# Selecting 512 tokens for each of 16 experts: a search and list building written anew, on one Trainium2 core

## The reference

```python
n_tokens = 8192; n_experts = 16; capacity = 512
logits = xn @ router_weight.T + router_bias
probs = softmax(logits, axis=-1)
_, idx = top_k(logits.T, capacity)
...
gates = take_along_axis(probs.T, idx, axis=1)
output = zeros.at[idx].add(y * gates)
gate_sums = zeros.at[idx].add(gates)
output = where(gate_sums > 0, output / gate_sums, output)
```

## Time and profile before

| | us |
|---|---|
| runs | 3954.75 (median of 3; 3950.32 to 3955.35) |
| profiled execution | 3953.91 |
| its span in the trace | 3951.6 |
| TensorE busy | 3623.9 (92%) |
| VectorE busy | 2290.3 (58%) |
| ScalarE busy | 1470.3 (37%) |
| POOL busy | 658.3 (17%) |

### The profile page before, as it was taken

The page is one execution under the profiler, slowest core; times in us unless marked ns, Lnnn a source line. Parts: engine busy times, 40 slices in busy tenths (PEclk is TensorE's granted clock), DMA queues, the critical chain, the costliest instruction groups (busy, mean ns, idle before and its releaser), DMA issues. The chain is left out here.

```text
span 3951.6 us, 57039 instructions
## 1 busy us (share of the span) xinstructions
PE 3623.9 (92%) x20457; PEld 2498.9 (63%) x20457; DVE 2290.3 (58%) x5022; ACT 1470.3 (37%) x2763; POOL 658.3 (17%) x852
## 2 busy tenths in 40 slices
PE   4899999999999999999999516999999999999995
PEld 3555556555555565555554306888888888888884
DVE  2576665765766757657666475444444444454456
ACT  1253443443434434435345102333333333333335
POOL 2022121121221211212211100011111111111113
PEclk7999999999999999999999755999999999999997
DMA  5234233234342332333421202344434334344448
GB/s 167 60 92 134 68 100 108 70 87 118 93 116 82 95 119 66 92 113 97 111 84 38 70 0 62 114 125 117 141 110 130 111 115 126 110 132 120 129 164 309
DMA packets 207410, 424.50 MB, mean 107 GB/s; under 512 B 45984, under 2 KB 49056, under 8 KB 198944
## 3 DMA queue, kind: packets, MB, share of 16 engines
q1 hardware_dynamic: 180464, 368.00, 30.3%
q0 software_dynamic: 14400, 35.14, 4.6%
q10 hardware_dynamic: 12288, 17.83, 1.6%
HBM read 246.75 MB, written 72.38 MB: 81 GB/s over the span
## 5 line engine op out<-in xcount | busy, mean ns | idle before, releaser
L833 ACT ACTIVATE probs<-scores_t 128x512 f32<-128x512 f32 (+3 forms) x1536 | 656.9, 496 | 574.9 <-PE scores_t L700 519.3
L1754 PE MATMUL m_ps_h<-m_tokens_t,m_w_parts 128*128 128x512 f32 x3072 | 740.8, 391 | 5.9 <-issue 4.3
L1754 PE MATMUL m_ps_y<-m_w_parts,m_hidden_parts 128*128 128x512 f32 x3072 | 736.7, 389 | 0.4
L1754 PEld LDWEIGHTS m_ps_h<-m_tokens_t,m_w_parts 128*128 128x128 f32 x3072 | 575.1, 188 | 126.7 <-issue 8.8
L1754 PEld LDWEIGHTS m_ps_y<-m_w_parts,m_hidden_parts 128*128 128x128 f32 x3072 | 575.9, 188 | 123.5 <-issue 3.7
L889 DVE CUSTOM_DVE_ANT_0 shared_banks<-shared_banks,mask_q_rows 128x128 f32<-128x128 f32 (+3 forms) x1024 | 477.5, 514 | 175.7 <-PE shared_banks L657 173.1
L657 PE MATMUL shared_banks<-k_operands,q_operands 96*128 96x512 f32 (+3 forms) x1536 | 509.0, 378 | 24.0 <-DVE natural L880 9.6
L700 PE MATMUL scores_t<-q_operands,k_operands 128*128 128x512 f32 (+3 forms) x1536 | 493.8, 371 | 33.0 <-ACT probs L833 25.7
L1572 ACT ACTIVATE m_hidden<-m_ps_h,m_b 128x512 f32<-128x512 f32 x256 | 176.6, 690 | 795.7 <-PE m_ps_h L1754 782.5
L657 PEld LDWEIGHTS shared_banks<-k_operands,q_operands 96*128 96x128 f32 x1536 | 278.6, 191 | 263.6 <-issue 121.9
L562 POOL TENSOR_SCALAR_AFFINE_SELECT probs<-probs 128x256 f32<-128x256 f32 x512 | 220.2, 432 | 1342.4 <-ACT probs L833 1341.9
(11 more groups left out here) (218 smaller groups left out, 3216.5 us busy)
## 6 DMA issues: line engine op xcount, KB each, us to landing
m_w_raw<-in_w1T SPq DMA_DIRECT2D x64, 1024.0 KB, 5.2
m_w_raw<-in_w2T SPq DMA_DIRECT2D x64, 1024.0 KB, 7.7
wqk_group<-scratch_wqk SPq DMA_DIRECT2D x32, 1024.0 KB, 5.5
q_operands<-natural SPq DMA_DIRECT2D x192, 128.0 KB, 2.6
k_operands<-natural SPq DMA_DIRECT2D x192, 128.0 KB, 3.0
q_operands<-natural SPq DMA_DIRECT2D x384, 64.0 KB, 2.0
k_operands<-natural SPq DMA_DIRECT2D x384, 64.0 KB, 2.0
natural<-in_xT SPq DMA_DIRECT2D x8, 2048.0 KB, 9.7
```

The lines of the kernel that those rows point to most:

```text
L833: act.activation(probs[:, slot_of(k, h // 2), h % 2, c0:HALF], st[:, (HG * k + h) % SCORE_BANKS, c0:HALF], ACT.Exp, scale=SCALE).then_inc( ...
L1754: mm = pe.matmul(bank, a, b, start=(first and n == 0), stop=(final and n == len(pairs) - 1))
```

## The change

All loops of the block are written out, and:

- **Loads.** Only `x` is loaded. Eight transposes of 128 by 128 of `x` take the place of the 64; they stand on TensorE behind the second count's product. The maximum and the subtraction read that layout with a stride of eight floats and stand behind the threshold on VectorE. `ones` moves from VectorE to POOL, whose large ramp (`iota_i`) moves behind `same` and `ident`.
- **Search.** `cand` holds the threshold so far and the three candidates. While the product runs, VectorE makes what the four would be next if the threshold stayed (`next_i`); then a compare whose accumulator is the number of candidates that hold (`keep`, `kept`), a cast to integer (`kept_i`), and a shift-or into the next four. The first step counts one candidate. The copies of `cid`, `pid` and `iota` stand under the products of the first two steps.
- **Lists.** Two experts share one chain of 64 products of 64 by 64, of which the two diagonal quarters are copied out by two ScalarE instructions; join, write and store handle two experts. The gates are made behind the one-hots of pairs 1 to 4, and SP issues their table behind the sixth pair's list.

```diff
-            sp.dma_start(logits[:], logits_dram[:, :]).then_inc(logits_in, 16)
-            sp.wait_ge(gates_ready, 1)
...
+            for it in range(PAIRS):
+                sp.wait_ge(list_ready, it + 1)
+                sp.dma_start(list_dram[2 * it:2 * it + 2, :].rearrange("a (h l) -> (a h) l", l=LO_N), lists[:, it % 2, :]
+                             ).then_inc(list_out[it % 2], 16)
+                if it == GATES_AT:
+                    sp.wait_ge(gates_ready, 1)
+                    sp.dma_start(table.rearrange("(c p) k -> p c k", p=P)[:, :, D:TABLE], gated[:]).then_inc(probs_out, 16)
...
+                for r in range(2):
+                    rows = slice(r * PAIR, (r + 1) * PAIR)
+                    act.activation(parts[rows, it % 2], ps_list[rows, it % 2, r * LO_N:(r + 1) * LO_N], ACT.Copy
+                                   ).then_inc(list_copied, 1)
...
-                    for n in range(NCH):
-                        mm = pe.matmul(ps_list[:, r, 0:LO_N], oh_tok[:, r, :, :, n].rearrange("p a h -> p (a h)"),
-                                       oh_col[:, r, :, n], start=(n == 0), stop=(n == NCH - 1))
...
+                for n in range(NCH):
+                    mm = pe.matmul(ps_list[:, b, 0:2 * LO_N], oh_tok[:, b, :, :, :, n].rearrange("p r a h -> p (r a h)"),
+                                   oh_col[:, b, :, :, n].rearrange("p r l -> p (r l)"),
+                                   start=(n == 0), stop=(n == NCH - 1))
+                mm.then_inc(list_mm, 1)
+                if it > 0:
+                    join_list(it - 1)
...
-                dve.tensor_tensor(keep[:], ps_cnt[:, 5:8], small[:, 3:4].to_broadcast([ROWS, 3]), ALU.is_ge
-                                  ).then_inc(d, 1)
-                for j in range(3):
-                    plain(dve, d, done + 3 + j, passed)
-                    dve.copy_predicated(thr[:], keep[:, j:j + 1].bitcast(U32), cand[:, j:j + 1]).then_inc(d, 1)
...
+                if i < SEARCHES - 1:
+                    dve.scalar_tensor_tensor(out=next_i[:], in0=steps_i[:], scalar=shift_of(i + 1),
+                                             in1=now[:, 0:1].to_broadcast([ROWS, 4]), op0=ALU.logical_shift_left,
+                                             op1=ALU.bitwise_or).then_inc(d, 1)
...
+                    then(dve.tensor_scalar(keep[:], ps_cnt[:, 5:8], small[:, 3:4], None, ALU.is_ge, ALU.add,
+                                           accum_out=kept[:]))
+                    then(dve.tensor_copy(kept_i[:], kept[:]))
+                then(dve.scalar_tensor_tensor(out=then_at, in0=kept_i[:].to_broadcast([ROWS, 4]), scalar=shift_of(i),
+                                              in1=next_i[:], op0=ALU.logical_shift_left, op1=ALU.bitwise_or))
...
+            scores = ps_lg[:].rearrange("p b (e s) -> p s b e", e=E_N)
+            tokens = lambda t: t.rearrange("p (s b) e -> p s b e", s=NB)
+            then(dve.tensor_reduce(red[:].rearrange("p (s b) -> p s b", s=NB), scores, AX.X, ALU.max))
...
+                dve.wait_ge(rows_ready, 2 * it + 2)
+                for r in range(2):
+                    dve.tensor_tensor(oh_tok[:, b, r, 1], oh_row[:, b, r], cid[:].unsqueeze(1).to_broadcast([P, HI_N, NCH]),
                                       ALU.mult).then_inc(onehots, 1)
+                if 1 <= it <= 4:
+                    dve.wait_ge(d, step[0])
+                    gate(it - 1)
+                if it > 1:
+                    write_list(it - 2)
```

More of the change, by code:

```diff
@@ L974, in build_selection @@
     HI_N = max(CAP // LO_N, 1)
+    PAIR = 2 * HI_N
     with ExitStack() as ctx:
@@ L1127, in _ @@
-            copy_list(E_N // 2 - 1, 1)
+                if it > 0:
+                    copy_list(it - 1)
+            copy_list(PAIRS - 1)
         @block.tensor
         def _(pe):
[L1131 to L1135, removed]
             group = same[:].rearrange("k e s -> k (e s)")
+            earlier = before[:].rearrange("k e s -> k (e s)")
@@ L1138, in _ @@
+            pe.wait_ge(made, 7)
             pe.wait_ge(counted, 1)
             pe.matmul(ps_cnt[:, 0:1], group, small[:, 0:1], start=True, stop=True).then_inc(grouped, 1)
-            with pe.Fori(0, SEARCHES) as i:
+            pe.wait_ge(counted, 2)
+            pe.matmul(ps_cnt[:, 5:6], group, counts[:, 0:1], start=True, stop=True).then_inc(grouped, 1)
+            pe.wait_ge(consts, 2)
+            pe.wait_ge(x_in, 16)
+            for b in range(TT):
+                mm = pe.transpose(ps_lg[:, b, :], x[:, b * P:(b + 1) * P], ident[0:ROWS, 0:ROWS])
@@ L1141, in _ @@
+            mm.then_inc(lg_full, 1)
+            for i in range(1, SEARCHES):
                 pe.wait_ge(counted, i + 2)
@@ L1212, in _ @@
-            then(dve.memset(bits[:], 1 << (BITS - 1)))
-            def search(i, done):
-                dve.tensor_tensor(cand[:], thr[:].to_broadcast([ROWS, 3]), bits[:], ALU.bitwise_or).then_inc(d, 1)
-                dve.wait_ge(d, done + 1)
-                for j, mark in enumerate((junk, gt, eq)):
-                    ins = dve.tensor_scalar(mark[:], xs[:], cand[:, j:j + 1].bitcast(F32), None, ALU.is_ge, ALU.add,
+            for i in range(SEARCHES):
+                now, then_at = cand[:, i % 2], cand[:, (i + 1) % 2]
+                for j in range(1 if i == 0 else 3):
+                    ins = dve.tensor_scalar(junk[:, j], xs[:], now[:, j + 1:j + 2].bitcast(F32), None, ALU.is_ge, ALU.add,
@@ L1230, in search @@
-                dve.wait_ge(d, done + 6)
-            PER = 6
-            search(0, step[0])
-            step[0] += PER
-            for j in range(3):
-                then(dve.memset(bits[:, j:j + 1], (j + 1) << (BITS - 3)))
-            first = step[0] - PER
-            with dve.Fori(1, SEARCHES) as i:
-                search(i, i * PER + first)
-            step[0] = first + SEARCHES * PER
-            then(dve.tensor_scalar(small[:, 7:8], thr[:].bitcast(F32), small[:, 2:3], None, ALU.mult))
@@ L1243, in _ @@
-            then(dve.tensor_scalar(gt[:], x[:], small[:, 7:8], None, ALU.is_gt, ALU.add, accum_out=small[:, 5:6]))
+                if i == 0:
+                    dve.wait_ge(made, 8)
+                    dve.tensor_copy(cid[:], cid_i[:])
+                    dve.tensor_copy(pid[:], pid_i[:])
+                if i == 1:
+                    dve.tensor_copy(iota[:], iota_i[:]).then_inc(pid_ready, 1)
+                if i < SEARCHES - 1:
+                    dve.scalar_tensor_tensor(out=next_i[:], in0=steps_i[:], scalar=shift_of(i + 1),
+                                             in1=now[:, 0:1].to_broadcast([ROWS, 4]), op0=ALU.logical_shift_left,
+                                             op1=ALU.bitwise_or).then_inc(d, 1)
+                else:
+                    dve.tensor_copy(next_i[:], now[:, 0:1].to_broadcast([ROWS, 4])).then_inc(d, 1)
@@ L1301, in _ @@
-            each(dve, run)
-            for r in range(2):
-                write_list(E_N // 2 - 1, r)
+                if 1 <= it <= 4:
[3 more added lines that the diff above has]
+                    write_list(it - 2)
+            write_list(PAIRS - 2)
+            write_list(PAIRS - 1)
 Z_OWN = 4
```

232 lines of the change are left out of this document (113 added, 119 removed).

## The result

| | before | after |
|---|---|---|
| runs, median of 4 each | 3953.18 us (3950.32 to 3955.35) | 3901.99 us (3900.64 to 3905.84) |
| ratio, 95% interval | | 0.9873 [0.9855, 0.989] |
| profiled execution, span | 3953.91, 3951.6 | 3901.82, 3900.1 |
| selection, from the load of x to the experts' first load | 219.45 | 171.62 |

Faster by 51.2 us, inside the range, 6 above the forecast. First the windows of the changed kernel, in the search and in the lists (columns as in the earlier trace rows).

A forecast was written before the change was run, and what follows sets the result against it. Selection stage bound by VectorE's dependent steps in the search and TensorE's small products at 1.2 GHz in the lists. Savings 16.8 + 22.0 - 0.3 + 19.5 = 58.0 us from 3953.91 give 3896 us, range 3889 to 3912.

The forecast's parts named there:

- Start-up: From the load of x to the search: x lands after 4.4 us, search begins at 2238.3; 16.8 us saved.
- Search: Threshold search: a step falls from 6.30 to 5.05 us, the whole from 100.83 to 78.8; 22.0 us saved.
- 0.37: Search: us per short instruction in the old loop; 0.19 to 0.27 was taken for straight-line code.
- Threshold to lists: Between search and lists: strided maximum costs 0.5 us beyond its wait, dropped waits return 0.1; -0.3 us saved in the sum.
- Lists: List products and end of stage: 54.3 us instead of 73.8, a pair with join 5.69; 19.5 us saved.
- 32 more columns at 1.2 GHz are 26.7 ns: Lists: a 64 by 64 product takes 86.5 ns, against 59.8 before, if only the moving side counts.
- the 0.9 us that I had put down for the gates: Lists: the gates hide under the products except some 0.9 us in which the one-hots' double buffer runs dry.
- the load hides under the product before: Lists: the wider stationary load adds no time; argued from old transposes at 109 ns each.
- loads are not hidden: Rival, lists: load and product add up to 113.2 ns, lists 67.1 us, kernel 3908.7 us; chance 0.25.
- VectorE became the bound: Rival, lists: products stay at 59.8 ns, one-hots set the pace, kernel 3894.0 us; chance 0.2 together with a faster clock.
- No product waited for the one before: Rival, lists, claimed the opposite: products don't pipeline, pitch 228 ns, 72.4 us more, kernel 3968.3 us; chance 0.03.
- The table behind the sixth list: End of lists: the gates' table takes 7.7 us to land, about when the last lists do; costed at nothing.

The follow-up runs named there:

- loads run: Changed kernel with the second copy of the logits loaded again, behind x, into a tile nobody reads: 3904.81 us.
- copies run: Changed kernel with the old compare, three predicated copies and new candidates back in the search from its second step, in straight-line code: 3910.45 us.
- two strips: Changed kernel, each pair's products unpaired to 32 by 32, alternating between two array strips: 3892.49 us; gates' table moved behind the fourth pair: 3890.20 us.
- packed kernel: Changed kernel with the one-hots stored with a chunk's columns side by side, the 64 by 64 products kept: 3921.57 us.
- four strips: Changed kernel with 32 by 32 products in four array strips, even and odd chunks apart, join of 128 rows, table behind fourth list: 3900.59 us.

## Why the prediction was right, and where not

- **Start-up**: right, and 1.1 low, since x landed in 3.3 us and not 4.4. The loads run settles it.
- **Search**: right: a step of 5.03 for 5.05, the short steps 0.26, 0.19 and 0.20 apart. For counts and product I had put 4.39 where the earlier trace rows have 4.45, without a reason; 4.38 came, which is luck, worth 0.9 us over 15 steps. That the loop and not the dependence had set 0.37 is shown by the copies run.
- **Threshold to lists**: the strided maximum took 1.20 us, not the 1.6 I priced, nearly all under the wait; and the four short passes that split the places start 0.61 apart, 0.73 before.
- **Lists**: the step that failed is "32 more columns at 1.2 GHz are 26.7 ns". I read the 59.8 ns of the earlier trace rows as 26.7 for 32 columns and a fixed rest, so that twice the columns would cost 86.5. There is no such rest: 56.4 ns for 32 columns, 111 for 64, some 1.75 ns a column when the columns lie 128 bytes apart and the products follow each other in one strip; from columns side by side 64 take 56.1. That is 27.2 ns times 512, 13.9 us; the lists came 12.8 later than forecast, as the 0.9 us that I had put down for the gates did not come (TensorE busy 50.00 of 50 us). What I argued beside it, that the load hides under the product before, was right. The Trainium skill's rule against the pairing ("TensorE: Matmul & The Clock Gate", "What overlaps and what doesn't") does not hold here: 64 loaded and 32 streamed cost what 64 and 64 do.
- **The rivals**: "loads are not hidden" gave 113.2 ns and 67.1 us for the lists, measured 113.7 and 67.08, and the sign I had named for it, 7.2 us per 64, came too (7.29 and 7.30). Its mechanism is wrong all the same: its sum would be 86.5 ns for 64 and 32, and 111.4 and 110.6 were measured. VectorE became the bound only in kernels with cheaper products, at best at 154.63 us of stage. No product waited for the one before.
- **The table behind the sixth list**: nothing, as forecast, by a narrow margin: 2389.70 and 8.6 are 2398.3, and the stage ends at 2399.24. With the faster two strips it cost 1.6.

That the total missed by 6 and not 10 us is luck: the 4.26 us lie outside the stage. Without them it would have been some 3906, inside the range only because that had taken in the 3908.7 of the rival with the loads.

## What to carry to other kernels

Before a product is made wider, divide the pitch of the present one by its columns, and look at how far apart the columns lie in memory: here a pitch well over one column a cycle was no fixed cost to be shared, and it grew with the width. A layout can serve two engines at once: here short runs of 2 values kept VectorE's rate and gave TensorE its own back, and runs of 4 nearly so at 0.50. And price a step in a loop by straight-line rows only if the loop goes.

## What the runs showed that I had not expected

- The clock rose where TensorE did less. In the changed kernel it is 0.50 with 50.00 of 50 us busy; with columns 4 bytes apart 0.74, 1.00 and 0.64 (0.74 and 0.64 are means of both levels) were granted in single pairs' products, with pauses of 1 to 2.8 us between them. Why is open; the packed kernel, with pauses of 6, had 0.50 in most of its stretches.
- Products in four strips slowed VectorE and ScalarE (the partition one-hots 1350 ns for 1142), though they write other buffers than the products read and POOL was idle. With two strips the first pass of the gates took 2316 ns for 1994, the one-hots kept their time. Products from columns side by side or 4 bytes apart slowed nobody. Where the engines met was not tried.
- Two strips gave 43.7 ns, four 28.9, one 56.4, all from columns 128 bytes apart; what shares out the reads among strips stays open.
